# Graph convolution over sorted edges: seed tables by a running sum, embedding products spread among the columns, and partition one-hots in two halves

## What is computed

```python
def gcn_conv(x, W, b, row, col, num_nodes):
    h = x @ W
    loop = jnp.arange(num_nodes)
    row_sl = jnp.concatenate([row, loop])
    col_sl = jnp.concatenate([col, loop])
    deg = segment_sum(ones_like(col_sl), col_sl, num_segments=num_nodes)
    dinv = rsqrt(maximum(deg, 1.0))
    norm = dinv[row_sl] * dinv[col_sl]
    msg = h[row_sl] * norm[:, None]
    out = segment_sum(msg, col_sl, num_segments=num_nodes)
    return out + b

h1 = gcn_conv(emb, W1, b1, row, col, 25000)      # 64 -> 128 features
lookup = gcn_conv(h1, W2, b2, row, col, 25000)   # 128 -> 64 features
return lookup[input]                             # input: 512 x 200
```

## Time and profile of the kernel before

| | us |
|---|---|
| median of 3 runs | 6868.01 |
| lowest, highest | 6863.18, 6872.12 |
| the profiled execution, its own time | 6869.0 |
| its span in the profile | 6867.3 |
| first gather starts | 786.6 |
| last gather of pass two starts | 5835.4 |
| busy: PE, DVE, ACT, POOL | 5034.4, 4014.0, 2327.5, 4539.2 |

### The profile page before, as it was taken

The page is one execution under the profiler, slowest core; times in us unless marked ns, Lnnn a source line. Parts: engine busy times, 40 slices in busy tenths (PEclk is TensorE's granted clock), DMA queues, the critical chain, the costliest instruction groups (busy, mean ns, idle before and its releaser), DMA issues.

```text
span 6867.3 us, 134775 instructions
## 1 busy us (share of the span) xinstructions
PE 5034.4 (73%) x27534; PEld 4382.0 (64%) x27535; DVE 4014.0 (58%) x13643; ACT 2327.5 (34%) x6633; POOL 4539.2 (66%) x4736
## 2 busy tenths in 40 slices
PE   6868898998999999888788888888888888000000
PEld 5634476776776777888788888888888888000000
DVE  8977798788788798566566555555555555000000
ACT  7957798688688688211000000000000011000000
POOL 0000377777777777777677777777777777677777
PEclk9989999899899899555555555555555555555555
DMA  0001111111111111111111111111111111111111
GB/s 14 0 17 40 28 24 25 26 25 25 26 25 25 27 25 25 30 39 39 33 26 26 26 26 26 26 26 26 27 26 26 35 39 39 44 53 53 53 53 52
DMA packets 184478, 210.98 MB, mean 31 GB/s; under 512 B 81356, under 2 KB 100182, under 8 KB 184336
## 3 DMA queue, kind: packets, MB, share of 16 engines
q0 software_dynamic: 151040, 154.97, 11.4%
q1 hardware_dynamic: 15280, 35.45, 1.4%
q10 hardware_dynamic: 18016, 19.05, 1.0%
HBM read 163.62 MB, written 45.54 MB: 30 GB/s over the span
## 4 chain that ended last, share of the span: by engine, by line
PE 36%; POOL 30%; issue 17%; DVE 7%; DMA 7%; DVEq 2%; ACT 0%; POOLq 0%; SPq 0%; ACTq 0%
PE ps L667 25%; POOL scratch L381 19%; POOL acc L414 11%; PE ps L571 10%; DMA scratch<-table,source 7%; DVE hi_onehot L840 2%; DVE acc L1046 1%; DVE place_i L1001 1%; DVE late L1025 1%; PE ps L720 1%; DVE late L1036 1%; DVE scratch L840 0%; DVEq L1044 0%; DVEq L854 0%; DVE prt_onehot L840 0%
## 5 line engine op out<-in xcount | busy, mean ns | idle before, releaser
L381 POOL DMA_INDIRECT scratch<-table,source x3920 | 3780.5, 964 | 2051.2 <-issue 1104.7
L667 PEld LDWEIGHTS ps<-scratch,late 128*128 128x128 f32 x19520 | 3751.6, 286 | 822.4 <-issue 657.5
L667 PE MATMUL ps<-scratch,late 128*128 x19520 | 3738.9, 369 | 574.5 <-SPq L340 341.7
L1046 DVE TENSOR_TENSOR acc<-acc,ps 128x128 f32 x4880 | 1358.2, 278 | 1378.6 <-PE ps L667 1345.0
L1036 DVE TENSOR_SCALAR late<-ramp,target 128x256 f32<-128x256 f16 x4148 | 1564.2, 377 | 149.0 <-issue 71.5
L467 ACT ACTIVATE late<-prt_onehot,scratch 125x128 f16<-125x128 f16 x4000 | 1236.4, 387 | 306.3 <-DVE prt_onehot L840 151.2
L571 PE MATMUL ps<-late 125*128 125x488 f16 x4000 | 1128.3, 375 | 35.8 <-DVE late L1025 32.9
L414 POOL DMA_INDIRECT acc<-lookup,scratch x800 | 755.1, 944 | 267.4 <-issue 243.4
L543 ACT ACTIVATE acc<-acc,dinv (+1 forms) x196 | 57.5, 340 | 2441.5 <-DVE acc L1046 2441.5
L1025 DVE TENSOR_SCALAR late<-ramp,tcol 125x488 f16<-125x488 f16 x2000 | 697.6, 358 | 48.9 <-PE ps L571 48.3
L571 PEld LDWEIGHTS ps<-late 125*128 125x128 f16 x4000 | 397.6, 119 | 146.2 <-DVE late L1025 60.8
(11 more groups left out here) (149 smaller groups left out, 1106.6 us busy)
## 6 DMA issues: line engine op xcount, KB each, us to landing
scratch<-table,source POOLq DMA_INDIRECT x3920, 2.5
out<-acc SPq DMA_DIRECT2D x40, 640.0 KB, 3.0
acc<-lookup,scratch POOLq DMA_INDIRECT x800, 2.4
table<-acc SPq DMA_DIRECT2D x49, 128.0 KB, 2.5
table<-acc ACTq DMA_DIRECT2D x49, 128.0 KB
lookup<-acc ACTq DMA_DIRECT2D x49, 128.0 KB
late<-embT ACTq DMA_DIRECT2D x47, 128.0 KB, 2.7
scratch<-edge_index SPq DMA_DIRECT2D x2, 976.6 KB
```

Of the source, the lines that this page charges most:

```text
L381: pool.indirect_dma_start(out=place, out_offset=None, in_=table[r], in_offset=bass.IndirectOffsetOnAxis(ap=source[:, t:t + 1], axis=0)).th ...
L667: last = pe.matmul(visit_ps[odd * W8 + k][:, n * FEAT:(n + 1) * FEAT], target_onehot[:, odd * W8 + k, n * P:(n + 1) * P], row, start=True, ...
L1046: dve.tensor_tensor(dst, dst, visit_ps[odd * W8 + k].rearrange("p (n f) -> p n f", f=FEAT), ALU.add).then_inc(visits_added, 1)
```

## The change

Four things change.

- **Base numbers.** The five running sums run ahead of the reciprocal, each behind the count copy of its own chunk. `seed` keeps the inclusive sum. Block ends are read from it with a stride, and a new small tile `shift` (490 numbers) holds what is to be added for each block. `seed_ranks` adds `shift` times 128 when it writes the seeds of a chunk into PSUM. The matrices `before`, `after` and `itself` become negative, so ranks count down from the end of a slot.
- **Embeddings.** TensorE has one of the four matmuls behind each of the columns 2 to 5. VectorE scales the group of the batch before, right behind the block one-hots. SyncE issues the loads, in turn with its stores.
- **Partition one-hots.** They are made in two halves of 512, with a column one-hot between them. ScalarE waits for each half by itself. `RANK` becomes 6. The same holds in `both`.
- Three weight tiles move into `lo_onehot`'s memory, and GpSimd clears three more small tiles at the start.

```diff
-        RANK = 5
+        RANK = 6
...
                 for s in range(GROUPS):
+                    if s + 2 < GROUPS:
+                        sp.wait_ge(emb_multiplied, s + 1)
+                        sp.dma_start(emb_sb[:, s % 2, :], embT[:, (s + 2) * EN:(s + 3) * EN]).then_inc(emb_loaded[s % 2], 16)
                     sp.wait_ge(emb_scaled, s + 3)
...
-            def sort_batch(i, k, load):
+            def sort_batch(i, k):
 
                 s, b = i * STEPS + k, k % 2
-                act.wait_ge(rank_step, s * RANK + RANK)
                 for j in range(W8):
+                    if j % (W8 // 2) == 0:
+                        act.wait_ge(rank_step, s * RANK + (RANK - 1 + j // (W8 // 2)))
                     scale_column(s, j, b)
-                    if load and j == W8 - 2:
-
-                        act.wait_ge(emb_multiplied, s + 1)
-                        act.dma_start(emb_sb[:, b, :], embT[:, bass.ds((s + 2) * EN, EN)]).then_inc(emb_loaded[b], 16)
...
                 rank_rest(s + 1)
-                pe.wait_ge(emb_loaded[b], i * 16 + 16)
-
-                pe.wait_ge(emb_scaled, s + 1)
-                for k in range(ET):
+                for j in range(2, W8):
+                    place_column(s, j)
+                    if j >= 2 + ET:
+                        continue
+                    if j == 2:
+                        pe.wait_ge(emb_loaded[b], i * 16 + 16)
+                        pe.wait_ge(emb_scaled, s + 1)
+                    k = j - 2
                     last = pe.matmul(emb_ps[b][:, k * FEAT:(k + 1) * FEAT], emb_sb[:, b, k * P:(k + 1) * P], w12[:, :],
                                      start=True, stop=True)
-                last.then_inc(emb_multiplied, 1)
-                for j in range(2, W8):
-                    place_column(s, j)
+                    if k == ET - 1:
+                        last.then_inc(emb_multiplied, 1)
...
+            step = chain(base_step)
+            dve.wait_ge(ramps_cast, 2)
+            for c in range(CHUNKS):
+                dve.wait_ge(counts_summed, c + 1)
+                step(dve.tensor_tensor_scan(seed[:, c, :], counts[:, c * SLOTS:(c + 1) * SLOTS], zeros_f[:, 0:SLOTS],
+                                            0.0, ALU.add, ALU.add))
             dve.wait_ge(root_taken, 1)
...
-            step(dve.tensor_reduce(flat, per_slot, AX.X, ALU.add))
...
-            step(dve.tensor_tensor(seed_flat, seed_flat, counts[:, :], ALU.subtract))
-
-            step(dve.tensor_tensor(flat_i, seed_slot[:, :, 0], flat, ALU.add))
+            step(dve.tensor_copy(tot_i, block_end))
...
-            step(dve.tensor_scalar(flat, flat, 0.0, None, ALU.is_gt))
+            step(dve.tensor_scalar(tot[:, :, 0:1], block_end[:, :, 0:1], 0.0, None, ALU.is_gt))
+            step(dve.tensor_tensor(tot[:, :, 1:NB], block_end[:, :, 1:NB], block_end[:, :, 0:NB - 1], ALU.is_gt))
...
-            step(dve.tensor_tensor(low_flat, end_flat, flat, ALU.subtract))
-            step(dve.scalar_tensor_tensor(seed_slot, low_flat.unsqueeze(2).broadcast_to([P, CHUNKS * NB, W8]), float(P),
-                                          seed_slot, ALU.mult, ALU.add))
+
+            step(dve.scalar_tensor_tensor(shift[:, :, :].rearrange("p c n -> p (c n)"), end_flat, -1.0 / P, flat, ALU.add, ALU.subtract))
...
                 block_onehots(s + 1)
+                if emb:
+
+                    dve.wait_ge(emb_multiplied, s)
+                    dve.tensor_tensor(acc[:, bass.ds((s - 1) * ET, ET), :], emb_ps[1 - b].rearrange("p (t f) -> p t f", f=FEAT),
+                                      dinv[:, bass.ds((s - 1) * ET, ET)].unsqueeze(2).broadcast_to([P, ET, FEAT]),
+                                      ALU.mult).then_inc(emb_scaled, 1)
                 column_onehot(s, 0, b)
...
-                partition_onehots(s + 1, 1 - b)
-                for j in range(4, W8):
+                partition_onehots(s + 1, 1 - b, 0)
+                column_onehot(s, 4, b)
+                partition_onehots(s + 1, 1 - b, 1)
+                for j in range(5, W8):
                     column_onehot(s, j, b)
```

More of the change, by code:

```diff
@@ L146, in build @@
         seed = sb("seed", [P, CHUNKS, SLOTS], F32)
+        shift = sb("shift", [P, CHUNKS, NB], F32)
         DW = max(CV, CHUNKS * NB)
@@ L365, in _ @@
             pool.iota(visit_no_i[:, :], pattern=[[1, VP]], base=0, channel_multiplier=VP).then_inc(ints_made, 1)
-            pool.wait_ge(ints_made, 7)
-            pool.affine_select(out=before[:, :], in_=ones[:, :], compare_op=ALU.is_gt, fill=0.0,
+            for triangle in (before, after, itself):
+                pool.memset(triangle[:, :], -1.0).then_inc(ints_made, 1)
+            pool.wait_ge(ints_made, 10)
+            pool.affine_select(out=before[:, :], in_=before[:, :], compare_op=ALU.is_gt, fill=0.0,
                                base=0, pattern=[[1, P]], channel_multiplier=-1).then_inc(triangles_made, 1)
-            pool.affine_select(out=after[:, :], in_=ones[:, :], compare_op=ALU.is_gt, fill=0.0,
+            pool.affine_select(out=after[:, :], in_=after[:, :], compare_op=ALU.is_gt, fill=0.0,
                                base=0, pattern=[[-1, P]], channel_multiplier=1).then_inc(triangles_made, 1)
-            pool.affine_select(out=itself[:, :], in_=ones[:, :], compare_op=ALU.is_equal, fill=0.0,
+            pool.affine_select(out=itself[:, :], in_=itself[:, :], compare_op=ALU.is_equal, fill=0.0,
                                base=0, pattern=[[1, P]], channel_multiplier=-1).then_inc(triangles_made, 1)
@@ L1113, in first_places @@
                 cast_places(s)
-                partition_onehots(s, 0)
+                for h in range(2):
+                    partition_onehots(s, 0, h)
             first_places(0)
@@ L1144, in _ @@
             seed_ranks(1)
-            sort_batch(*divmod(CB - 1, STEPS), emb=False)
+            sort_batch(*divmod(CB - 1, STEPS))
             decode(0)
```

82 lines of the change are left out of this document (36 added, 46 removed).

## The result

| | before | after |
|---|---|---|
| median, us | 6869.5 (4 runs, one more than above) | 6825.1 (4 runs) |
| lowest, highest | 6863.18, 6872.12 | 6824.65, 6826.0 |
| the profiled execution, its span | 6869.0, 6867.3 | 6825.35, 6823.5 |
| first gather starts | 786.6 | 765.2 |
| last gather of pass two starts | 5835.4 | 5791.9 |

A forecast was written before the change was run, and what follows sets the result against it. GpSimd's gather queue was taken to bound the kernel. Base numbers 19.5, sort batches 64, minus 0.4, gathers 10: 93 us off 6869.0 gives 6776, median 6775; own range 6748 to 6796, wider range 6745 to 6808.

The forecast's parts named there:

- What bounds the kernel: GpSimd runs one gather queue from 786.6 us to the end; its start and the time per gather set the end.
- Base numbers: VectorE's stretch ahead of the sort: removed operations and earlier scans save 19.5 us, bounds 18.5 and 20.
- The sort ring without the spreading: Chunk 0 sort batches with the embedding at its old price: 5.84 us each instead of 6.61.
- rival 2: Sort batches: VectorE's early wait for the embedding delays the reduction, batch stays at 6.5 us, time 6833; chance 0.05.
- The price of a pair: TensorE in sort batches: an embedding matmul behind a column costs 0.13 to 0.20 us, 0.26 in the solid block.
- Rival 1: Sort batches: the embedding's weight loads do not hide, batch 5.84 us, sum 67 us, time 6801; chance 0.14.
- Gathers: While gathers run, two half-length partition one-hots hold them less than one whole: 10 us less.
- by chance alone: Gathers beside VectorE: by chance, loss goes with squared instruction length, giving partition one-hots 42 of the 70 us.
- The square law: Gathers beside partition one-hots: 2 x 0.42^2 against 0.68^2, so two halves lose a quarter less.
- The other bound: Gathers beside the halves: the loss grows with the partition one-hots' busy time, 6 us more.
- Rival 3: Gathers and batches fall out of step, nearly all partition holds vanish: 32 us more saved, time 6743; chance 0.08.
- Rival 4: In 200 batches beside the gathers both halves hold a gather for their whole length, time 6883; chance 0.02.

The follow-up runs named there:

- Spread with 128 rows: The changed kernel with the embedding matmuls, still one behind each of columns 2 to 5, padded with zeros from 64 to 128 rows; 6767.33 us.
- Quarters: The changed kernel with each half of the partition one-hots made by two instructions of 256, back to back; 6840.76 us.
- solid block: The changed kernel with the four embedding matmuls together ahead of column 2 again, all else kept; 6788.22 us.
- block halves: The changed kernel with embedding matmuls padded to 128 rows and also the block one-hots (784 wide) made in two of 392; 6746.83 us.

## Why the prediction was half right

**What bounds the kernel: right.** The time moved by the first gather's start plus the change in the gathers' busy time. After: 21.4 + 20.9 = 42 of 44 us. Spread with 128 rows: 79.1 + 21.2 = 100 of 101. Quarters: 23.5 + 4.6 = 28 of 28.

**Base numbers: right.** 20.3 us against 19.5, a little past the upper bound of 20. The two strided inputs of L922 cost what one does (1.03 us for 485 numbers, 1.04 for 490 with one). The kernel with the new base numbers alone confirms the term: 18.8 us at the first gather.

**The sort ring without the spreading: right.** Batch 5.84 forecast, 5.85 measured with the solid block. The early wait of VectorE (rival 2) did no harm: VectorE still stands 1.37 us for the embedding (L1132 above), as it stood 1.38 in the earlier trace rows, but nothing queues behind it now that TensorE needs at once: from the rank matmuls "before" to "after" it is 1.56 us as before.

**The price of a pair: the step that failed.** I took 0.13 to 0.20 us for an embedding matmul behind a column, from the visits of the earlier trace rows, and called the solid block's 0.26 the upper end. It costs 0.47. The nearest row for a mix of the two was of 128 rows against 125, and this pair has 64. I noted that the rows differ and concluded that loads would be shorter; what mattered was whether they run ahead at all. With 128 rows the step holds as written (0.58 for column and pair, batch 5.39 against the 5.33 to 5.59 of the text). In the sum that is 49 x 1.28 (6.58 less the forecast 5.3) = 63 us, of which the gathers gave 12 back and the base numbers 1. That the kernel with 128 rows, at 6767, is so near the forecast 6775 is partly luck: its sort gains 4 us less than forecast, its gathers 11 more.

**Rival 1: right mechanism, price too low.** The loads do not hide, but I gave it the solid block's price, 5.84 a batch. In the solid block only two changes of rows are paid, spread out there are eight. It gave 6801; the kernel took 6825. I spoke of the rule in the Trainium skill (TensorE: Matmul & The Clock Gate, The mechanism), that a load overlaps a running matmul only when the row groups differ. By that rule no load here would run ahead, at 64, 96 or 128 rows. The same section of the Trainium skill also lets a load into the background weight buffer go ahead, and no run here shows which buffer a load goes to. The rows show loads of 96 and 128 rows starting 0.21 us ahead under a matmul of 125, and only those of 64 waiting. The measurement decides: the rule on row groups alone does not hold, and my "the trace speaks against it" was true of the rule and false of this kernel.

**Gathers: 22 us, forecast 10, inside the bounds.** What failed is "by chance alone": hits are not by chance, and the loss does not go with the square of the length. Gathers and VectorE hold each other and so fall in step (82 hits with wholes, 69 with halves), and each hit loses what is left of one instruction from 0.2 us after its start (0.475 us of 0.68, 0.207 of 0.41). The square law gave 10 for halves and had quarters cost the same as halves, but quarters lost 16 of these 22 us. The other bound was worked out wrongly too: a loss of 42 us that grows with the busy time, from 0.68 to 0.84, grows by 10 and not by 6.

**Rival 3** (nearly all holds vanish by phase) did not come in this kernel; the kernel with block halves went part of that way (31 hits left). **Rival 4** (both halves hold a gather each) did not come.

## What to carry over

Before small matmuls are put between others, compare the number of rows: on these rows a change from 125 to 64 and back costs 0.29 us, and with zeros up to 96 or 128 rows that price is gone (0.17 us a pair instead of 0.47), so gather such matmuls in one block or pad them. A price from a nearby row is only good if what makes it cheap there (a load that runs ahead) holds here; look at the PEld rows for that. Where a periodic stream of VectorE work holds a stream of gathers, shorten the longest two-input instruction first and measure: the two engines hold each other, so their steps shift with every edit, and here that moved the result by 10 to 20 us either way (quarters 16 us worse, block halves 14 us better than expected).

## What the runs showed of the hardware

- TensorE's weight loads of 96 and 128 rows (fp32) start 0.21 us ahead and those of 125 rows (fp16) behind them 0.11 us ahead, under the matmul before. Next to a 64-row matmul neither the load to it nor the load from it runs ahead: the loader is idle for 0.40 us ahead of each of the four 64-row loads, and a change to 64 rows and back costs 0.29 us on the matmuls.
- A four-matmul fp32 block of 64 rows between matmuls of 125 is not cheaper than one of 128 rows: 1.46 us against 1.17 from the last rank matmul to column 2.
- A gather (0.94 us by itself) that starts 0.08 us after a VectorE instruction with two SBUF inputs takes 1.42 us beside one of 0.68 us and 1.15 beside one of 0.41. Between two of 0.41 us that stand back to back it gets going (63 of 64 gathers); between two of 0.28 us only some do (67 of 94), and a gather that starts 0.13 us ahead of such a pair is held over both (1.43 us).
- The hold goes both ways: VectorE's target one-hots (L1036 before) take 0.51 us when they start 0.5 to 0.6 us into a gather and 0.35 when they start in its first 0.4 us, and in the hits end 0.11 us after the gather. So the two fall in step: 82 gathers started 0.07 to 0.08 us into a partition one-hot, where chance gives 21 in twice that stretch.
- A strided fp32 read costs VectorE the same for one strided input (1.04 us for 490 numbers) and for two (1.03 us for 485); without a stride 490 numbers take 0.67 us (L930 of the kernel after).
